# Edge masks of a graph network: two whole-array loads per mask, issued by ScalarE, in place of one small load per group

## The reference, cut to what matters

```python
x = _layernorm(x + _L0_gnn_ref(x, edge_index, edge_weight, ...))   # GCN: weighted sum over a node's edges
x = _layernorm(x + _L1_gnn_ref(x, edge_index, ...))                # PNA: max, min, mean, std over a node's edges
x = _layernorm(x + _L2_gnn_ref(x, edge_index, edge_type_8, ...))   # attention over a node's edges
x = _layernorm(x + _L3_gnn_ref(x, edge_weight, src, dst, ...))     # max over a node's messages
```

## Time and profile before

| what | value |
|---|---|
| median of 3 runs | 3927.42 us (3923.71 to 3927.47) |
| the profiled execution's own time | 3923.91 us |
| its span, first to last instruction | 3922.2 us |
| mean granted TensorE clock | 0.899 |
| busy share PE, DVE, ACT, POOL | 80%, 76%, 59%, 68% |
| dense pass | 375.7 to about 1463.8 us |
| first edge layer (`gcn_edges`) | 1472.4 to about 2017 us |

### The profile page before, as it was taken

How to read it: one execution, slowest core, us unless ns; L and a number is a source line. 1 busy time by engine, 2 the same in 40 slices (tenths; PEclk the granted TensorE clock), 3 DMA queues, 4 the chain that set the end, 5 groups by cost and what they waited for, 6 DMA issues and landing times. The chain is left out here.

```text
span 3922.2 us, 55046 instructions
## 1 busy us (share of the span) xinstructions
PE 3144.1 (80%) x11677; PEld 2053.1 (52%) x11677; DVE 2971.8 (76%) x7760; ACT 2315.5 (59%) x5112; POOL 2668.5 (68%) x2681
## 2 busy tenths in 40 slices
PE   5401799999999976888879999978888888678776
PEld 3200455555555544555549999974444444344443
DVE  3694899999999965777758999968999999433332
ACT  3200799999999974555533343336888888433333
POOL 4775799988889867777734444435666666477776
PEclk8755899999999997888879999999999999788887
DMA  7200333333333323444432223232222222233322
GB/s 238 77 2 7 103 125 130 123 132 121 130 124 127 128 87 112 124 130 130 126 78 86 87 89 92 87 79 62 79 78 78 78 78 78 51 87 86 83 79 56
DMA packets 250729, 377.44 MB, mean 96 GB/s; under 512 B 66186, under 2 KB 102755, under 8 KB 250649
## 3 DMA queue, kind: packets, MB, share of 16 engines
q1 hardware_dynamic: 186240, 275.69, 21.5%
q0 software_dynamic: 51328, 75.23, 8.7%
q10 hardware_dynamic: 13081, 25.69, 2.0%
HBM read 209.35 MB, written 171.27 MB: 97 GB/s over the span
## 5 line engine op out<-in xcount | busy, mean ns | idle before, releaser
L206 POOL TENSOR_TENSOR dn_rstd<-dn_var,w_minus_half 128x4 f32<-128x4 f32 x300 | 306.5, 1025 | 86.3 <-DVE dn_var L191 86.3
L1402 POOL DMA_INDIRECT p_src<-table_x,e_src x200 | 218.3, 1091 | 100.9 <-issue 54.4
L1402 POOL DMA_INDIRECT m_src<-table_x,e_src_first x200 | 194.5, 972 | 75.1 <-issue 47.2
L1223 PEld LDWEIGHTS d_pair<-w_gru_both,d_xT 128*128 128x128 f32 x800 | 196.6, 327 | 92.7 <-ACT d_xT L1261 90.5
L2194 POOL DMA_INDIRECT out_rows<-m_x,e_out_first x200 | 201.2, 1006 | 63.7 <-issue 59.7
L1402 POOL DMA_INDIRECT a_src<-table_x,e_src x200 | 200.0, 1000 | 61.2 <-issue 50.4
L612 POOL DMA_INDIRECT scratch_node_row<-o_own,e_out x200 | 196.2, 981 | 64.2 <-issue 63.3
L1223 PE MATMUL d_pair<-w_gru_both,d_xT 128*128 128x256 f32 x800 | 230.2, 432 | 11.8 <-ACT d_xT L1261 9.1
L1402 POOL DMA_INDIRECT g_own<-in_x,e_dst x200 | 188.7, 944 | 70.6 <-issue 66.7
L1402 POOL DMA_INDIRECT g_src<-in_x,e_src x200 | 188.9, 945 | 69.8 <-issue 59.7
L1676 POOL TENSOR_TENSOR pn_rstd<-pn_var,w_minus_half 128x4 f32<-128x4 f32 x50 | 52.1, 1042 | 262.1 <-DVE pn_var L191 262.1
(11 more groups left out here) (456 smaller groups left out, 10356.6 us busy)
## 6 DMA issues: line engine op xcount, KB each, us to landing
table_x<-d_x SPq DMA_DIRECT2D x300, 256.0 KB, 2.1
d_x<-in_x SPq DMA_DIRECT2D x99, 256.0 KB, 2.7
out_rows<-d_x SPq DMA_DIRECT2D x97, 256.0 KB
s_x<-in_x ACTq DMA_DIRECT2D x31, 768.0 KB, 5.8
table_x<-g_x SPq DMA_DIRECT2D x50, 256.0 KB, 2.8
scratch_post<-g_post SPq DMA_DIRECT2D x50, 256.0 KB, 2.1
p_rc<-scratch_rcount SPq DMA_DIRECT2D x50, 256.0 KB, 3.3
p_post<-scratch_post SPq DMA_DIRECT2D x50, 256.0 KB, 2.7
```

Source lines behind the costliest of these rows:

```text
L206: pool.tensor_tensor(self.rstd[s][:], self.var[s][:], minus_half[:], ALU.pow).then_inc(self.rooted[s], 1)
L1223: mm = pe.matmul(pair[s][:, 2 * t * P:2 * (t + 1) * P], xT[s][:, t:GROUP:TPG], W.gru_both[:], start=True, stop=True, skip_group_check=True)
L1402: pool.indirect_dma_start(out=self.rows[s][:, t * P:(t + 1) * P], out_offset=None, in_=self.table, in_offset=bass.IndirectOffsetOnAxis(ap= ...
```

## The change

`e_keep` is allocated before `dense_pass` and filled there: ACT's stream begins with two transfers, one with 25 of the mask's 51 rows (128 x 12,800 values, 25,600 bytes in each partition), one with the other 26 (128 x 13,312 values, 26,624 bytes in each). `e_low` is filled in the same way at the start of ACT's stream in `gcn_edges`. SP waits for the completion of each at the end of the block that issued it. The step MASKS is gone, with its wait on the scan, and the scan waits for no mask any more.

```diff
+def spread_mask(eng, mask, rows, plan, landed):
+
+    half = plan.AG // 2
+    for lo, hi in ((0, half), (half, plan.AG)):
+        flat = rows[lo:hi, :].rearrange("(o g) f -> o (g f)", o=1)
+        eng.dma_start(mask[:, lo * GROUP:hi * GROUP], flat.to_broadcast([P, (hi - lo) * GROUP])).then_inc(landed, 16)
...
 def dense_pass(nc, A, D, W, Ed, plan):
...
                 sp.wait_ge(st4[s], 16 * sum((i * S + s) * GROUP < N for i in range(rounds)))
+            sp.wait_ge(keep_landed, 32)
...
         @block.scalar
         def _(act):
+            spread_mask(act, Ed.keep, D["keep"], plan, keep_landed)
+
             def step(k, s, i):
                 if k == COPY:
...
 def gcn_edges(nc, A, D, W, Ed, plan):
...
         @block.scalar
         def _(act):
+            spread_mask(act, Ed.low, D["low"], plan, low_landed)
+
             def step(k, s, i):
                 if k == WEIGH_SRC:
...
                 if k == SCAN:
-                    wait(dve, masked[s], 32 * i + 32)
                     wait(dve, src_turned[s], i + 1)
...
-                if k == MASKS:
-                    wait(sp, scanned[s], i)
-                    mem.settle(sp)
-                    for mask, row in ((Ed.keep, D["keep"]), (Ed.low, D["low"])):
-                        sp.dma_start(pos(mask, g), row[bass.ds(g, 1), :].to_broadcast([P, GROUP])).then_inc(masked[s], 16)
...
                 sp.wait_ge(post_stored[s], 16 * rounds)
+            sp.wait_ge(low_landed, 32)
...
-    with nc.cleanup_on_exit():
-        dense_pass(nc, A, D, W, Ed, plan)
-    with nc.cleanup_on_exit():
-        Ed.add_masks(nc, plan)
+        Ed.add_keep(nc, plan)
+        with nc.cleanup_on_exit():
+            dense_pass(nc, A, D, W, Ed, plan)
+        Ed.add_low(nc, plan)
```

More of the change, by code:

```diff
@@ L584, in __init__, with add_keep, add_low @@
         self.att = mem.sb("e_att", [P, plan.ET])
-    def add_masks(self, nc, plan):
+    def add_keep(self, nc, plan):
+        self.keep = Mem(nc).sb("e_keep", [P, plan.EP], BF16)
+    def add_low(self, nc, plan):
         self.low = Mem(nc).sb("e_low", [P, plan.EP], BF16)
-        self.keep = Mem(nc).sb("e_keep", [P, plan.EP], BF16)
+def spread_mask(eng, mask, rows, plan, landed):
[3 more added lines that the diff above has]
+        eng.dma_start(mask[:, lo * GROUP:hi * GROUP], flat.to_broadcast([P, (hi - lo) * GROUP])).then_inc(landed, 16)
 class OwnRows:
@@ L1158, in dense_pass @@
      x3_turned, x3_copied, hidden3, relued, product, residual, rows_made, st1, st2, st3, st4) = (sem[name] for name in names)
-    began = mem.sem("d_began")
+    began, keep_landed = mem.sem("d_began"), mem.sem("d_keep_landed")
     (LOAD, TURN, COPY, LAYERS, SQUARE0, SUM0, ROOT0, SCALE0, ST1, COMBINE, SQUARE1, SUM1, ROOT1, SCALE1, ST2, BIAS, SQUARE2,
@@ L1435, in gcn_edges @@
     gown = Gather(mem, "go", S, Ed.dst0, A["x"], own)
-    (weighed, own_weighed, kept, src_turned, own_turned, masked, scanned, summed, made, mixed, x1_turned, x1_copied, post_made,
+    (weighed, own_weighed, kept, src_turned, own_turned, scanned, summed, made, mixed, x1_turned, x1_copied, post_made,
      plain_copied, amped, posted, stored, post_stored) = (mem.sems("g_" + n, S) for n in (
-        "weighed", "own_weighed", "kept", "src_turned", "own_turned", "masked", "scanned", "summed", "made", "mixed", "x1_turned",
+        "weighed", "own_weighed", "kept", "src_turned", "own_turned", "scanned", "summed", "made", "mixed", "x1_turned",
         "x1_copied", "post_made", "plain_copied", "amped", "posted", "stored", "post_stored"))
-    began = mem.sem("g_began")
+    began, low_landed = mem.sem("g_began"), mem.sem("g_low_landed")
     table, post_table = groups_of(D["x1"]), groups_of(D["post"])
@@ L1443, in gcn_edges @@
     column = lambda ap, i, s, t: ap[:, bass.ds((i * S + s) * TPG + t, 1)]
-    (SRC0, SRC1, SRC2, SRC3, OWN0, OWN1, OWN2, OWN3, MASKS, WEIGH_SRC, WEIGH_OWN, KEEP_OWN, TURN_SRC, TURN_OWN, SCAN, SUM,
-     PRODUCT, OUTER, MOMENTS, ROOT, NEWTON, LAST, STORE, TURN1, COPY1, POST, PLAIN, MIX, STORE_POST) = range(29)
-    AT = (0.5, 3, 5.6, 8.1, 1.8, 4.3, 6.8, 9.3, 0, 11.7, 13.1, 18, 13, 14.5, 14.1, 15.6, 17.1, 19.3, 20.7, 22.9, 23.3, 24.9,
+    (SRC0, SRC1, SRC2, SRC3, OWN0, OWN1, OWN2, OWN3, WEIGH_SRC, WEIGH_OWN, KEEP_OWN, TURN_SRC, TURN_OWN, SCAN, SUM,
+     PRODUCT, OUTER, MOMENTS, ROOT, NEWTON, LAST, STORE, TURN1, COPY1, POST, PLAIN, MIX, STORE_POST) = range(28)
+    AT = (0.5, 3, 5.6, 8.1, 1.8, 4.3, 6.8, 9.3, 11.7, 13.1, 18, 13, 14.5, 14.1, 15.6, 17.1, 19.3, 20.7, 22.9, 23.3, 24.9,
           29.7, 26.7, 27.6, 29.2, 34.5, 36.4, 39.3)
```

## The result

The changed kernel takes 3935.76 us in the median of 8 runs (3933.37 to 3940.44), the kernel before 3925.54 us (3923.08 to 3927.47, 8 runs). The ratio is 1.0027, with a 95% interval of 1.0016 to 1.0038: slower by about 10 us. The forecast was 3936 us, 9 us more than before.

A forecast was written before the change was run, and what follows sets the result against it. The prediction took DVE to bound dense and POOL's gather issue to pace the first edge layer. Its terms, 0 + 0 + 0 + 9 + 0 = +9 us on 3927.42, gave 3936 us, range 3922 to 3941.

The forecast's parts named there:

- What bounds the kernel: Dense middle: DVE, busy 676.82 of 700 us; first edge layer: POOL's gather issue, 97% of the 10.24 us pace.
- rival C: Edge layer gains from a fifth fewer bytes: -14 us, with dense's +9 a net -5 (3922, same); chance 0.12.
- Removed issues, the scan's wait, a fifth of the bytes: Edge layer: SP's 100 issues, DVE's scan wait and 256 KB a group go away, all hidden today: 0.
- Two issues on ACT: Head of dense and edge layer: two issues of 0.4 to 0.5 us, hidden before ACT's first work: 0.
- The mask in dense: Dense start: 8 rows of `d_x` per DMA engine each wait for one mask packet, delaying the pass: +9 us.
- it just fits: Dense start: second load lands at about 395.4, before ACT needs its transposed tile at 396.5.
- rival B: Dense start: mask rows move in pieces, or SP's rows go first; +1.4 to +5, 3929 to 3932, same; chance 0.25.
- Rival E: Nothing moves, as ACT reaches its issue after SP's rows are through: +0 to +1, 3928; chance 0.07.
- The mask in the edge layer: Edge layer start: each gather waits for at most one mask row, about 1.1 us, hidden: 0 to 1, taken as 0.
- The sum: Whole kernel: 0 + 0 + 0 + 9 + 0 = +9 us, on the median 3927.42 + 9 = 3936.
- Rival A: Dense start: a mask row moves as one packet, alternating with SP's rows; +8.6 to +13.4, 3936 to 3941; chance 0.50.
- Rival D: Dense loses more, or the edge layer's clock pattern changes, costing 13 us more: 3949; chance 0.06.

The follow-up runs named there:

- behind_and_4k: Changed kernel with `e_keep` issued by SP behind its first two `d_x` loads and `e_low` in 13 transfers with 4,096-byte rows; 1.0010 of the kernel before.
- rows_of_4k: Changed kernel with each mask in 13 transfers with rows of 4,096 bytes in place of two transfers; 4433.32 us, 1.0010 of the kernel before.

## Why the prediction was right, point by point

**What bounds the kernel.** Right. The middle of dense kept its pace, and the 6.2 us lost at its start are in its end (+6.1). One sum in it is off: the pause after a gather is put at 0.30 us, where the rows it names give 0.32. With 0.323, 8 gathers make 10.14 us, and POOL's 3.9 us for ACT in 39 groups add 0.10: that is the whole 10.24. So 0.10 us a group were left for rival C, 5 us in all, not 0.29 and 14.

**Removed issues, the scan's wait, a fifth of the bytes: 0.** Right. SP's wait grew by 52 us over the same stretch, and the step between scans stayed (10.26 against 10.24 us). Rival C, a gain of up to 14 us, is refuted by this step, and behind_and_4k, which carries all of the removal and little of the cost, is not faster. The step is the stronger evidence, since the edge layer of the two chips is slower than POOL's pace for reasons that are open.

**Two issues on ACT: 0.** Right for the change (0.85 and 0.82 us, ahead of waits of 15.72 and 29.70 us). With 13 issues it would have been wrong in dense, as rows_of_4k shows. That the 7.852 us of the earlier trace rows were a full queue, as the prediction reads it, no run shows; the 13 issues in dense took 0.34 to 0.76 us each.

**The mask in dense: +9.** The mechanism was right and the term mis-sized: it measured 6.2 us. The price of a turn was right (1.03 us against 1.08). Wrong was the count, "each of the 8 rows that a DMA engine has of `d_x` waits for one packet of the mask". Four rows pass before the mask's packets begin to take full turns, so about five turns are paid, the closing packet's among them, and not eight or nine. The first transposes came at 384.95, not at 387, the wait was 10.46 us, not 13. The landing of the second load, "it just fits", was right. The rule of the Trainium skill that was weighed ("DMA: Bandwidth & Descriptors", section "Queues, rings and completion order": turns by packet) agrees with the one-for-one counts of long rows, if what the profile counts as a packet is the page's packet. That page's section "SWDGE vs HWDGE vs iDMA" says that a packet is preferably at most 4096 bytes; in these transfers rows of 25,600 and of 52,224 bytes went as one packet each. With that rival B is refuted. Rival E, nothing moves, had a true core: the first four rows do get through.

**The mask in the edge layer: 0.** This is the step that failed: "A gather is issued every 1.25 us, and each waits for at most one mask row, about 1.1 us. ACT's first scaling moves from 1483.15 to about 1484.3." It moved by 10.2 us against the first gather. A gather sends two packets on each DMA engine, its rows and the closing one (so near half of the 320 above are under 512 bytes), and each waits its turn: from 1486 to 1498 us 191 packets of the mask and 190 of the gathers passed, 12 on an engine, which is 6 gathers in the time in which POOL issues 9 or 10. The wait isn't one turn but a queue that grows until the mask is through. In the first 6 us the gathers sent even less than turns would give them (16 packets against 78), and why is open. What saved the sum is what the step relied on besides, POOL's lead of two slots: POOL stood only 2.11 + 1.24 us, the layer's last scan came 522.3 us after the first gather in place of 517.4, and the block ended 2.1 us longer. The 0 became +2.1, not +10. The 2.1 us are of the size of POOL's two waits, but stand in one profile of each kernel, and the edge layers on the experiments' chips vary too much to test them.

**The sum.** +9 against +10.2 between the medians. The forecast of 3936 us looks nearer than that because it was added to 3927.42, and the kernel before had 3925.54 in the median of its 8 runs. By terms, in the profiled executions: dense +6.1 for 9, edge layer +2.1 for 0, and +0.5 in the prelude, -1.0 in attention and +2.5 in the last layer, where nothing was changed. The first two errors, -2.9 and +2.1, nearly cancel (8.2 against 9), and that is luck. The other three sum to +2.0; they come from one execution of each kernel, and whether they belong to the change is open. On the experiments' chips the last layer varies by 38 us without an order in what was changed.

**The chances.** Rival A, with half of the weight, is what happened by its mechanism; its price for dense, +8.6 us or more, was too high (6.1). Rival D, another pattern of clocks, did not show: 0.83 and 1.00 in the two windows, as before.

## What to carry to other kernels

Before a large transfer is moved to an idle queue, ask how long its longest contiguous row is, and who loads something small at the same time. With rows of 26 KB and more, each packet of the small load, closing packets too, waited for one whole row of the large one, once the first few were through, and a stream of small gathers fell behind until the large transfer was through. What took the cost away at the start of dense was to issue the large transfer in the same queue right behind the urgent loads; rows of 4 KB made it smaller at both starts, where the issuing engine has the time for more issues. And look first whether the small loads that it replaces were waited for at all: here they weren't, and without them nothing was faster.

## What the runs showed of the hardware that was not expected

- In the first 6 us after the first gather only 16 packets of gathers passed against 78 of the mask (125 in the kernel before). Turns alone don't explain it. With rows of 4 KB it was 44 against 478. What holds the gathers is open.
- A broadcast row of 52,224 bytes moved as one packet of 2.0 us (144 packets for 6.68 MB), and SP's packets went between two such rows one at a time (80 against 80).
- Where the mask was issued 0.01 us behind `d_x`, four rows of `d_x` on each engine got through before the mask took its full turns (64 packets against 16), with rows of 26 KB and of 52 KB alike.
- Three queues took turns one for one for one (177, 176 and 177 packets in 12 us), whatever the size of their packets.
- The same kernel took 3925 us in the main comparison and about 4435 us on each of the experiments' two chips. The difference sits in the prelude, the first edge layer and the last layer; the other three blocks take the same time to within 2 us.
